# Layer two's attention in another order with its own bank for turned attention, and the first feed-forward layer written out group by group

## The reference

```
act_quant(x)    = clip(round(x * s), -128, 127) / s,   s = 127 / max|x| over the row
weight_quant(w) = clip(round(w * s), -1, 1) / s,       s = 1 / mean|w|
h   = act_quant(layernorm(x)) @ weight_quant(w1).T     # 128 -> 512
h   = silu(depthwise_conv1d(h, 3 taps over the tokens) + b)
out = act_quant(h) @ weight_quant(w2).T                # 512 -> 128
```

```
Sim    = h@w1 + (c@w2).T + (h*w3)@c.T + b        # 128 x 128
A      = softmax(Sim, over c);  hq = A @ c
h_bar  = softmax(max(Sim, over c), over tokens) @ h    # one row, for all tokens
out    = concat(h, hq, h*hq, h*h_bar) @ W_qv + b_qv
```

## Time and profile before

| | |
|---|---|
| median of 3 runs | 1749.2 us (1742.07 to 1757.42) |
| the profiled execution | 1753.31 us, its span 1751.5 us |
| TensorE (PE) busy, share of the span | 1434.0 us, 82% |
| VectorE (DVE) busy | 901.2 us, 51% |
| ScalarE (ACT) busy | 510.1 us, 29% |
| GpSimd (POOL) busy | 413.7 us, 24% |
| mean granted clock of TensorE | 0.869 |
| the chain that ended last, by engine | PE 27%, DVE 2%, POOL 1% of the span |

### The profile page before, as it was taken

The page is one execution under the profiler, slowest core; times in us unless marked ns, Lnnn a source line. Parts: engine busy times, 40 slices in busy tenths (PEclk is TensorE's granted clock), DMA queues, the critical chain, the costliest instruction groups (busy, mean ns, idle before and its releaser), DMA issues. The chain is left out here.

```text
span 1751.5 us, 26351 instructions
## 1 busy us (share of the span) xinstructions
PE 1434.0 (82%) x8869; PEld 909.0 (52%) x8869; DVE 901.2 (51%) x2554; ACT 510.1 (29%) x1195; POOL 413.7 (24%) x713
## 2 busy tenths in 40 slices
PE   4798886885688885897778669666699999999998
PEld 2577663443467673665677547444344443444443
DVE  4565646886356552433354433375544465455535
ACT  1455552111366652222443223243010110111001
POOL 2665710000466520000133322262000000000000
PEclk8698988997599877999575679888799999999999
DMA  6665650000667636700000011123222022022110
GB/s 179 170 160 136 147 132 1 1 0 7 170 154 165 155 87 241 312 0 8 23 19 20 21 46 56 46 66 109 97 97 103 1 102 103 25 78 103 60 43 12
DMA packets 134171, 151.33 MB, mean 86 GB/s; under 512 B 12150, under 2 KB 117942, under 8 KB 128806
## 3 DMA queue, kind: packets, MB, share of 16 engines
q1 hardware_dynamic: 127494, 142.28, 27.6%
q0 software_dynamic: 3296, 6.76, 1.3%
q10 hardware_dynamic: 3264, 0.79, 0.2%
HBM read 99.33 MB, written 49.48 MB: 85 GB/s over the span
## 5 line engine op out<-in xcount | busy, mean ns | idle before, releaser
L2596 DVE TENSOR_TENSOR l3f_weighted_T<-l3f_w_e,l3f_xnT 128x512 f32<-128x512 f32 x128 | 88.4, 691 | 129.8 <-PE psum L2347 115.0
L2347 PE MATMUL psum<-l3f_weighted_T,w_l3f_q 128*128 128x512 f32 x256 | 133.7, 604 | 16.2 <-DVE l3f_weighted_T L2596 14.4
L2347 PE MATMUL psum<-l3f_weighted_T,w_l3f_k 128*128 128x512 f32 x256 | 131.6, 596 | 0.0
L2347 PE MATMUL psum<-l3f_weighted_T,w_l3f_v 128*128 128x512 f32 x256 | 131.5, 595 | 0.0
L710 DVE TENSOR_REDUCE l1x_minus_max<-psum 128x4 f32<-128x512 f32 x128 | 85.9, 687 | 81.0 <-PE psum L373 79.7
L2356 PE MATMUL psum<-l3f_weighted_T,w_l3f_o 128*128 128x512 f32 x256 | 124.4, 624 | 1.7 <-DVE l3f_weighted_T L2596 1.7
L710 DVE TENSOR_REDUCE l0x_minus_max<-psum 128x4 f32<-128x512 f32 x128 | 85.4, 686 | 66.5 <-PE psum L373 65.9
L2596 DVE TENSOR_TENSOR l3f_weighted_T<-l3f_w_e,l3f_oT 128x512 f32<-128x512 f32 x128 | 88.4, 692 | 57.3 <-PE psum L2356 30.0
L531 ACT ACTIVATE l0x_probsT<-psum 128x512 f32<-128x512 f32 x128 | 73.6, 595 | 57.2 <-PE psum L386 49.8
L111 POOL TENSOR_TENSOR l3f_ln_rstd<-l3f_ln_mean_var,eps 128x4 f32<-128x4 f32 x8 | 1.9, 243 | 355.5 <-DVE l3f_ln_mean_var L104 355.5
L531 ACT ACTIVATE l1x_probsT<-psum 128x512 f32<-128x512 f32 x128 | 73.7, 593 | 36.4 <-PE psum L386 26.9
(11 more groups left out here) (480 smaller groups left out, 3034.5 us busy)
## 6 DMA issues: line engine op xcount, KB each, us to landing
l3f_w_e<-l3f_weights_scratch SPq DMA_DIRECT2D x32, 1024.0 KB, 4.6
sorted_x<-zeros SPq DMA_DIRECT2D x1, 16896.0 KB, 59.0
l0x_k_scratch<-l0x_k_parts SPq DMA_DIRECT2D x24, 384.0 KB, 3.8
l0x_k_stack<-l0x_k_scratch SPq DMA_DIRECT2D x16, 576.0 KB
l0x_q_stack<-l0x_q_scratch SPq DMA_DIRECT2D x48, 192.0 KB
l1x_k_scratch<-l1x_k_parts SPq DMA_DIRECT2D x24, 384.0 KB, 4.6
l1x_k_stack<-l1x_k_scratch SPq DMA_DIRECT2D x16, 576.0 KB
l1x_q_stack<-l1x_q_scratch SPq DMA_DIRECT2D x48, 192.0 KB
```

The lines of the kernel that those rows point to most:

```text
L2347: ins = pe.matmul(bank[:, :], w[name][:, e, :], xe[:, e % 2, :], start=(e == 0), stop=(e == NE3 - 1))
L2596: dve.tensor_tensor(xe[:, e % 2, :], wE[:, g % 2, e, :], src, ALU.mult).then_inc(s_xe, 1)
```

## The change

In `layer0_ffn` the hardware loop goes, and all eight groups are written out. Normalise and the rounding steps move from VectorE to ScalarE (Identity with a scale and a bias per partition; the bias of the steps is the rounding constant in a tile of its own), for which POOL makes a `shift` with two more operations. ScalarE also takes the absolute value of each block behind its Silu (Abs), and VectorE takes the maximum of two, of two, and of those two, in three operations of 512 columns in place of the reduction. xn and the scales get two buffers. TensorE turns the next group's quantised input before the last of its four convolutions.

In `layer2` the turned probabilities get bank 2, and the experts' count and the router's output share bank 7. VectorE takes the token maximum and scales the probabilities ahead of the update, and chooses the experts ahead of the mixing weights. TensorE turns xn of s+1 behind the turn of h, and the router comes before the token probabilities. ScalarE empties xnT behind the token exponential.

```diff
 def layer0_ffn(nc, k):
...
+        magic = sb("magic", [P, 1], F32)
+        xn = sb("xn", [P, 2, GS, P], F32)
...
+        habs = sb("h_abs", [P, NHB, T], F32)
+        h2 = sb("h_absmax_of_two", [P, 2, T], F32)
...
         @block.tensor
...
+            turn_q(0)
+            pe.wait_ge(s_prep, 7)
+            for n in range(NHB - 1):
+                convolve(0, n)
+            turn_q(1)
+            convolve(0, NHB - 1)
+            for t in range(NG):
+                if t + 1 < NG:
+                    convolve(t + 1, 0)
+                turn_absmax(t)
+                if t + 1 < NG:
+                    convolve(t + 1, 1)
+                spread(t)
+                if t + 1 < NG:
+                    convolve(t + 1, 2)
+                if t + 2 < NG:
+                    turn_q(t + 2)
+                if t + 1 < NG:
+                    convolve(t + 1, 3)
+                down(t)
 
         @block.scalar
...
+            def normalise(g):
+                act.wait_ge(s_shift, g + 1)
...
+                for c in range(GS):
+                    ins = act.activation(xn[:, g % 2, c, :], k.x_sb[:, seq(g * GS + c)], ACT.Identity,
+                                         bias=shift[:, g % 2, c:c + 1], scale=rstd[:, g % 2, c:c + 1])
+                ins.then_inc(s_xn, 1)
+
+            def steps(g):
+                act.wait_ge(s_qs, g + 1)
...
+                for c in range(GS):
+                    ins = act.activation(xr[:, c, :], xn[:, g % 2, c, :], ACT.Identity, bias=magic[:, :],
+                                         scale=qs[:, g % 2, c:c + 1])
+                ins.then_inc(s_xr, 1)
...
+            def silu(g, n):
+                act.wait_ge(s_conv, g * NHB + n + 1)
...
+                act.activation(hT[:, g % 2, n, :], bankH[n % 2][:, :], ACT.Silu,
+                               bias=w["l0f_cb"][:, n:n + 1]).then_inc(s_h, 1)
+                act.wait_ge(s_h, g * NHB + n + 1)
+                if g >= 1:
+                    act.wait_ge(s_h2, 2 * g - 1 + n // 2)
+                act.activation(habs[:, n, :], hT[:, g % 2, n, :], ACT.Abs).then_inc(s_abs, 1)
+
+            normalise(0)
+            steps(0)
+            normalise(1)
+            xqT_out(0)
+            steps(1)
...
+            for t in range(NG - 1):
+                if t + 2 < NG:
+                    normalise(t + 2)
+                silu(t + 1, 0)
+                if t + 2 < NG:
+                    steps(t + 2)
+                silu(t + 1, 1)
+                silu(t + 1, 2)
+                if t + 2 < NG:
+                    xqT_out(t + 2)
+                silu(t + 1, 3)
 
         @block.gpsimd
...
+                step(pool.tensor_tensor(rs, mv[:, :, 1], k.eps[:, :], ALU.add))
+                step(pool.tensor_tensor(rs, rs, k.minus_half[:, 0:GS], ALU.pow))
+                step(pool.tensor_tensor(sh, mv[:, :, 0], rs, ALU.mult))
+                pool.tensor_scalar(sh, sh, -1.0, None, ALU.mult).then_inc(s_shift, 1)
...
         @block.vector
...
+            def larger_of_two(t, i):
+                dve.wait_ge(s_abs, t * NHB + 2 * i + 2)
+                if t >= 1:
+                    dve.wait_ge(s_hm, t)
+                dve.tensor_tensor(h2[:, i, :], habs[:, 2 * i, :], habs[:, 2 * i + 1, :], ALU.max).then_inc(s_h2, 1)
...
+            moments(1)
+            scale_of_x(0)
+            quantise(0)
+            round_weights()
+            scale_of_x(1)
+            quantise(1)
+            moments(2)
+            larger_of_two(0, 0)
+            for t in range(NG):
+                larger_of_two(t, 1)
+                larger_of_four(t)
+                if t + 2 < NG:
+                    scale_of_x(t + 2)
+                row_scales(t)
+                if t + 2 < NG:
+                    quantise(t + 2)
+                quantise_h(t)
+                if t + 1 < NG:
+                    larger_of_two(t + 1, 0)
+                if t + 3 < NG:
+                    moments(t + 3)
+                update(t)
 
 def layer2(nc, k):
...
-        bankX, bankS, bankK, bankA, bankO, bankX2, bankM, bankL = (k.bank(i) for i in range(8))
+        bankX, bankS, bankAT, bankA, bankO, bankX2, bankM, bankR = (k.bank(i) for i in range(8))
+        bankL, bankK = bankR[:, 0:GS * NE2], bankR[:, 256:256 + GS * NE2]
...
             def turn_attn(g):
                 pe.wait_ge(s_attn, g + 1)
-                pe.wait_ge(s_hw, min(g + 2, NG))
-                for c in range(GS):
-                    ins = pe.transpose(bankX[:, seq(c)], attn[:, c, :], k.ident[:, :])
+                if g >= 1:
+                    pe.wait_ge(s_at, g)
+                for c in range(GS):
+                    ins = pe.transpose(bankAT[:, seq(c)], attn[:, c, :], k.ident[:, :])
                 ins.then_inc(s_atp, 1)
...
             def route(g):
...
                     pe.wait_ge(s_sh, g)
+                    pe.wait_ge(s_pos, g)
...
             for s in range(last_step):
-                if s + 1 < NG:
-                    turn_xn(s + 1)
                 if s < NG:
                     similarity(s)
...
                 if 2 <= s < NG + 2:
                     turn_h2(s - 2)
+                if s + 1 < NG:
+                    turn_xn(s + 1)
                 if s < NG:
                     turn_attn(s)
-                    token_probs(s)
                 if 2 <= s < NG + 2:
                     route(s - 2)
                 if s < NG:
+                    token_probs(s)
                     attend(s)
                     weigh_tokens(s)
...
         @block.scalar
...
             for s in range(last_step):
-                if s + 1 < NG:
-                    xnT_out(s + 1)
                 if s < NG:
                     exps(s)
                 if 2 <= s < NG + 2:
                     hT2_out(s - 2)
                 if s < NG:
                     token_exp(s)
+                if s + 1 < NG:
+                    xnT_out(s + 1)
+                if s < NG:
                     attnT_out(s)
...
         @block.vector
...
                 if 3 <= s < NG + 3:
                     positions(s - 3)
+                if s < NG:
+                    token_max(s)
+                    normalise(s)
                 if 1 <= s <= NG:
                     update(s - 1)
                     stats2(s - 1)
                 if s < NG:
-                    normalise(s)
-                    token_max(s)
                     token_total(s)
                     token_probs_out(s)
                 if 2 <= s < NG + 2:
                     shifted(s - 2)
+                    choose(s - 2)
                 if s < NG:
                     mix_weights(s)
-                if 2 <= s < NG + 2:
-                    choose(s - 2)
-                if s < NG:
                     h_times_a(s)
```

239 lines of the change are left out of this document (122 added, 117 removed).

## The result

The changed kernel takes 1699.14 us (median of 4 runs, 1698.27 to 1701.69). The kernel before had one more run beside it, and its median of four is 1753.31 us (1742.07 to 1759.71). The profiled execution has a span of 1696.6 us, 54.9 less than before, and a mean granted clock of 0.883 for 0.869.

What follows compares the result with a forecast made beforehand. VectorE's string of work was taken to bound the first feed-forward layer, with TensorE waiting for the maxima; layer two's TensorE waited for scaled probabilities. 21 + 15 = 36 us off the 1749.2 median gave 1713 us, range 1696 to 1731.

Steps and rivals of the forecast that it cites:

- TensorE becomes the bound of the feed-forward layer, 13.6 us a group: First feed-forward layer: VectorE falls to about 11.1 us, TensorE's 13.4 us becomes the bound; five spacings give -18.5 us.
- The stall of 0.3 us: First feed-forward layer: the maxima's turn comes after 3.8 us, TensorE has 3.5 us of work meanwhile.
- Less than 13.4 it can't be: First feed-forward layer: TensorE's unchanged 13.4 us of work as the floor for a group.
- The start: First feed-forward layer: +2.0 us from POOL's added operations and slower normalise and steps, 0.5 back in the first group.
- VectorE's string of work is the loop: First feed-forward layer before the change: VectorE, busy 14.6 us a group, sets the loop; TensorE waits for the maxima.
- The unrolling at nothing: First feed-forward layer: writing out the loop costs nothing; 1 us a group if instruction cover is lacking.
- Layer two, probabilities done 7.2 us after the scores, token probabilities at 9.9, attend at 10.4, then held by h_bar: Layer two's step: the new order takes 17.9 us against 20.3; -15 us in sum, clock kept as it was.
- Rival A: Layer two: the clock goes up, -13 us over seven steps, 1700 us in total; chance 0.12.
- Rival B: First feed-forward layer: stall really over 1 us, so the clock keeps falling; +7, 1720 us; chance 0.15.
- Rival C: Layer two: wait moves to h_bar or token total, a step gains 0.5 us, not 2; +11, 1724 us; chance 0.15.
- Rival D: First feed-forward layer: Abs or Identity forces eight ScalarE table loads a group at 1.28 us; 1752 us; chance 0.04.
- the clock's rule: TensorE: throttled by default, activity releases it; by it layer two's denser order would make the sum about 13 us lower.

Runs made afterwards that it cites:

- the better order: Changed kernel, layer two: VectorE scales probabilities before positions, takes token total before moments; ScalarE writes turned attention before turned rows: 1680.31 us (0.9610).
- the last run: The better order with four unread 128x128 products per step of layer two, all ahead of the token scores: 1674.72 us (0.9586).

## Why the prediction was right

Forecast were 1713 us and a range of 1696 to 1731; 1699.14 lies inside, 3 us above its lower end. The gain was 54 us where 36 were forecast. The mechanism of each half was right, and two terms of the sum were too small, layer two's above all; 5.8 us came from stages that the change doesn't touch, which is luck.

- **TensorE becomes the bound of the feed-forward layer, 13.6 us a group:** 13.11, at 100% busy and a clock of 1.00. The stall of 0.3 us did not come: update, two maxima and the hop end at 342.6, just as the convolution does, and the maxima are turned at 342.65 with no idle time. "Less than 13.4 it can't be" was wrong: that figure is busy time of a group with two waits, and the last product ahead of a wait counts with its whole length. The turn of the input (L839) counts 0.61 us there, while in the changed kernel the next product starts 0.44 us behind it; the convolution's last pair counts 1.01, for 0.85 to the next start. Those two make up the 0.3 us. The start cost +0.8 us for +1.5, the last two groups gave 5.3 for 4. Together -25.4 for -21. ScalarE's 9.03 us a group stands against 9.2, Abs with 0.63 against 0.65, VectorE's 11.2 against 11.1.
- **The reading that VectorE's string of work is the loop** was only half true. Taking 1.8 us of work from it, with the reduction left, gained 0.2 us a group; what stands between the update and TensorE's turn of the maxima, 3.65 us of reduction for 1.4 us of maxima, was the cost, and the clock was about 44% of it (1.7 of 3.9 us). The prediction also named one wait of TensorE in a group, that for the maxima, where the trace has a second of 0.85 us, for ScalarE's copy of the turned input.
- **The unrolling at nothing:** shown, 0.9989 (0.9962 to 1.0016), 2.4 us in the stage of one execution.
- **Layer two, probabilities done 7.2 us after the scores, token probabilities at 9.9, attend at 10.4, then held by h_bar:** 6.4, 8.8, 9.1 and a wait of 0.35 us for h_bar. The order of events is the forecast one, the token total is what is late next (0.89 us), and the wait that I moved to h_bar is there. But each event is earlier by 0.8 to 1.3 us, since the output product turns to full clock before its end and attend takes 1.35 us for 2.05. Steps 3 to 6 took 16.1 us for the forecast 17.85, and steps 1 and 2 gave 5.6 us for 2.3. This is the term that was mis-sized, 24 us for 15: I kept the clock of layer two as it was. By the timeline of one step, Rival A, at 0.12, is most of what was missing in steps 3 to 6: of 1.75 us a step, 0.8 lie ahead of the scaled probabilities and 0.5 to 0.7 in attend and weigh, where the same products run faster. That is a reading; the runs with added products show what the clock is worth in the changed kernel, not what it added to the change. For the 3.3 us of steps 1 and 2 I have no such reading. Rival A's argument against, that the narrow products stand right before the scores, holds for the scores, which still take 2.05 us, and for no more.
- **Rival B** (clock still falling in the feed-forward layer) fell at 1.00. It would have come with the reduction left in place, whose groups read 0.90.
- **Rival C** (the wait only moves): it does move, to the token total and h_bar, 1.2 us of the 3. With VectorE's order alone, at 1.1 and 1.7 us, it moves almost whole, and yet the step gains 1.7 us, not the rival's 0.5. TensorE's order, with ScalarE's and the bank, brings the two down to 0.71 and 0.89 us.
- **Rival D** (table reloads): one load of 1.28 us in the stage. The Trainium skill (ScalarE: Activation LUTs, Table sets) has Abs in every set; the trace now agrees.
- **What is left, 5.8 us,** is from unedited stages, two of which differ by up to 16 us each between the fourteen profiled executions, all with the same code there.
- **Slips of the prediction's sums:** steps 3 to 6 took 78.8 us before, not 79.2, so the same working gives 7.4 for 7.8; and from A to C with 5 us each way is 1695 to 1729, not 1696 to 1731. Neither changes the outcome.

**On the clock's rule.** The runs with added products show what the clock is worth: 1.8 us a step in the changed kernel and 1.5 in the better order, for work that nobody reads. The Trainium skill (TensorE: Matmul & The Clock Gate, Part 1) says that the gate is set by how busy TensorE has been. With a wait of 2.17 us in front, as in the reduction's trace, it agrees. In the last run it doesn't, as far as "busy" is what the profile counts: 100% busy and 0.75 granted (869.55 to 883.40).

## What to carry to other kernels

Price a wait of TensorE twice, as itself and as the slow products behind it, and when an order removes one, count the clock that comes back; here that was 1.7 of 3.9 us in one stage and, by the timeline of one step, most of an unforeseen 1.75 us a step in the other. Look for what stands between the last producer and TensorE's next use, not for the engine with the most work: the same load on VectorE gave groups of 17.05 and 13.9 us. When moving one step earlier makes another the late one (here the token total behind the moments), move that one as well; with two other moves beside it that was worth 2.4 us a step more.

## What the runs showed of the hardware

- Products that nobody reads, in TensorE's waits, made three kernels faster in the stage they were put in: steps of 14.3 for 16.1 us, of 12.16 for 13.68, groups of 15.4 for 17.05.
- TensorE can be busy without a gap in the profile and still be granted 0.75 (13.85 of 13.85 us); among the products ahead of the fall were those of 128x8, 4x4 and 128x1.
- The same code of the first attention ended anywhere from 258.0 to 273.8 us into the span in fourteen profiled executions. Where a gain of a few us in one stage is at stake, its own window says more than the total.
